# The feed-forward's first two tiles of x loaded, normalised and quantised inside the preparation of the matrices, on one core of Trainium2

## The reference, cut to what matters

```python
mod = (silu(c) @ wmod).reshape(2, 6, 1, -1)
sa, ca, ga, sb, cb, gb = (mod[:, i] for i in range(6))
gb = (2 * (gb >= 0) - 1) * maximum(abs(gb), 0.25)
...                                            # attention: x = x + ga * attn(...)
h = layernorm(x) * (1 + cb) + sb
x = x + gb * ffn(h, w_gate, w_up, w_down)

def fp4_quant_dequant(x):                      # blocks of 16 along the last axis
    scale = maximum(max(abs(xb)) / 6.0, 1e-12)
    return grid[searchsorted(mid, abs(xb / scale))] * sign(xb) * scale

def fp4_linear(x, w):
    return einsum('bsk,nk->bsn', fp4_quant_dequant(x), fp4_quant_dequant(w))

def ffn(x, w_gate, w_up, w_down):
    gate, y = fp4_linear(x, w_gate), fp4_linear(x, w_up)
    return fp4_linear(silu(gate) * y, w_down)
```

## Time and profile before

| | us |
|---|---|
| median of 3 runs | 4038.29 (4036.18 to 4048.62) |
| the profiled execution's own time | 4013.47 |
| its span, first to last instruction | 4011.7 |
| preparation of the matrices, in its span | 2453.0 to 2578.5 |
| first product of the loop | 2599.71 |
| mean granted TensorE clock | 0.966 |

### The profile page before, as it was taken

One profiled execution on the slowest core, in us unless ns is written; L12 is line 12 of the kernel. 1 busy time (PEld: TensorE's weight loads), 2 busy tenths in 40 slices (PEclk: granted clock), 3 DMA queues, 4 the chain that ended last, 5 costly groups with the idle time before them and its releaser, 6 DMA issues. The chain is left out here.

```text
span 4011.7 us, 151421 instructions
## 1 busy us (share of the span) xinstructions
PE 3637.0 (91%) x63808; PEld 2365.8 (59%) x63808; DVE 3342.2 (83%) x7592; ACT 1742.8 (43%) x3510; POOL 863.6 (22%) x687
## 2 busy tenths in 40 slices
PE   4999999999999999999999984099999999999998
PEld 3777767777777676676776762044444444444443
DVE  4788888787888888888888867689999999999997
ACT  2444434434445354443443523344444444444443
POOL 1121222122222221222212210022222222222221
PEclk7999999999999999999999997599999999999999
DMA  4000000000000000100000013322333333333322
GB/s 122 13 25 29 20 25 29 19 30 24 25 30 19 25 29 20 34 20 25 30 19 25 24 71 108 69 72 76 85 87 75 89 82 80 89 75 86 85 77 76
DMA packets 359968, 204.57 MB, mean 51 GB/s; under 512 B 299761, under 2 KB 300401, under 8 KB 359281
## 3 DMA queue, kind: packets, MB, share of 16 engines
q1 hardware_dynamic: 359280, 194.66, 17.7%
HBM read 89.49 MB, written 33.55 MB: 31 GB/s over the span
## 5 line engine op out<-in xcount | busy, mean ns | idle before, releaser
L1618 PE MATMUL fbank<-gT,xqT 128*128 128x464 f16 (+1 forms) x2304 | 491.2, 363 | 124.7 <-DMA xqT<-xq 123.6
L950 DVE COPY_PREDICATED Am<-pick,banks 128x64 f32<-128x64 uint8 (+2 forms) x1792 | 461.7, 258 | 127.4 <-DVE Am L950 12.3
L782 POOL TENSOR_TENSOR raw_up<-raw_up,raw_gate 128x1024 f32<-128x1024 f32 x128 | 315.6, 2466 | 1160.5 <-DVE raw_up L832 1160.5
L1618 PE MATMUL fbank<-uT,xqT 128*128 128x464 f16 (+1 forms) x2304 | 487.7, 361 | 0.0
L1627 PE MATMUL fbank<-dT,hqT 128*128 128x512 f16 x2112 | 469.2, 381 | 8.2 <-DMA hqT<-hq 8.2
L535 PE MATMUL banks<-raw_up,raw_gate 128*128 128x256 f32 x2048 | 456.8, 381 | 2.3 <-DVE xxx L845 2.3
L1618 PEld LDWEIGHTS fbank<-gT,xqT 128*128 128x128 f16 x2304 | 221.8, 98 | 373.2 <-DMA xqT<-xq 117.2
L535 PEld LDWEIGHTS banks<-raw_up,raw_gate 128*128 128x128 f32 x2048 | 389.2, 191 | 67.8 <-issue 17.0
L1618 PEld LDWEIGHTS fbank<-uT,xqT 128*128 128x128 f16 x2304 | 225.4, 98 | 230.9
L1627 PEld LDWEIGHTS fbank<-dT,hqT 128*128 128x128 f16 x2112 | 207.1, 98 | 257.7 <-DMA hqT<-hq 8.5
L436 PE MATMUL banks<-rcol,kvar 32*32 32x80 f32 x8192 | 335.2, 236 | 25.9 <-issue 25.7
(11 more groups left out here) (225 smaller groups left out, 7118.2 us busy)
## 6 DMA issues: line engine op xcount, KB each, us to landing
raw_scale<-in_L_attn_x SPq DMA_DIRECT2D x32, 512.0 KB, 3.6
xres<-in_L_attn_x SPq DMA_DIRECT2D x32, 512.0 KB, 3.6
x_after_attention<-xres SPq DMA_DIRECT2D x32, 512.0 KB, 2.8
xl<-x_after_attention SPq DMA_DIRECT2D x64, 256.0 KB, 2.7
xr<-x_after_attention SPq DMA_DIRECT2D x64, 256.0 KB, 2.6
out<-xr SPq DMA_DIRECT2D x64, 256.0 KB, 2.3
raw_gate<-in_L_ffn_w_gate SPq DMA_DIRECT2D x1, 2816.0 KB, 11.7
raw_up<-in_L_ffn_w_up SPq DMA_DIRECT2D x1, 2816.0 KB, 18.7
```

Of the source, the lines that this page charges most:

```text
L782: nc.gpsimd.tensor_tensor(xf[:, j % NXF].rearrange("p g b t -> p (g b) t"), xf[:, j % NXF].rearrange("p g b t -> p (g b) t"), hT[:, :, :, ...
L950: nc.vector.copy_predicated(dst, mask, src).then_inc((done or A_step).sem, 1)
L1618: last = nc.tensor.matmul(GU[2 * pair + t][:, 0:w], xqT[:, u, a, g, :], W[:, b_, g, lo_:hi_], start=(k == 0), stop=(k == 3 * G - 1))
```

## The change

The first steps of tiles 0 and 1 move from the loop's block into the preparation's block, into each engine's order there. The tiles of x get places in rows of `raw_gate` and `raw_up` that are no longer read at that point, as the preparation's temporary tiles are still in use. The whole preparation moves behind the functions it now calls, so the plain diff shows it as removed and added; what differs is this. VectorE's two copies of c also move behind the first two divisions of gate.

```diff
-        xl = sb("xl", [P, 2, C])
-        passed = sb("passed", [P, C])
-        hx, mx = sb("hx", [P, C]), sb("mx", [P, C])
...
+        xl, hx, passed, mx = early.gate[:, G:G + 2], early.gate[:, G + 2], early.gate[:, G + 3], early.gate[:, G + 4]
+        full_x = early.gate[:, G + 5].bitcast(F16).rearrange("p (a n) -> p a n", a=2)
+        xq = early.gate[:, G + 6].bitcast(F16).rearrange("p (a n) -> p a n", a=2)
+        xqT = early.up[:, 2 * G:2 * G + 2].rearrange("p r n -> p (r n)").bitcast(F16).rearrange("p (u a g t) -> p u a g t", u=2, a=2, g=G)
+        q16x = early.up[:, 2 * G + 2].bitcast(F16)[:, 0:C]
...
 # preparation, SP, behind the transpose of item n
+                        if n == KF - 1:
+                            sp.wait_ge(a_done.sem, KF)
+                            for u in range(2):
+                                sp.dma_start(xl[:, u], x1[u, 0:P, :]).then_inc(xl_loaded[u].sem, 16)
+                        if n == 2 * KF - 2:
+                            sp_xT(sp, 0, 0)
 # preparation, ScalarE, item n
+                        if n == 2 * KF:
+                            act_grid(act, 0, xstep, hx[:], mx[:], xgrid_done)
+                            act_full(act, 0, C, s16x, xs_done, full_x, xfull_done, xlow_done)
...
+                        if n == KF + 4:
+                            act_stats(act, 0, 0, 0)
+                        if n == KF + 6:
+                            act_ln(act, 0, 0)
+                            act_stats(act, 0, 1, 1)
+                        if n == 2 * KF + 1:
+                            act_ln(act, 1, 1)
 # preparation, GpSimd
+                    pool.wait_ge(consts.sem, 1)
                     for t in range(3):
+                        if t == 2:
+                            pool.wait_ge(row_done.sem, 2)
+                            pool_x(pool, 0, 0)
                         pool.wait_ge(wmax_done.sem, t + 1)
                         nc.gpsimd.partition_all_reduce(wall[:, t:t + 1], wmax[:, t:t + 1], P, bass.bass_isa.ReduceOp.max).then_inc(all_max.sem, 1)
+                    pool_x(pool, 1, 1)
 # preparation, VectorE
-                    dve.wait_ge(c_ready.sem, 1)
-                    for b in range(B):
-                        last = V.tensor_copy(c_b[:, b], c_s[:, :, b:b + 1].to_broadcast([P, G, P]))
-                    last.then_inc(cb_ready.sem, 1)
+                    def spread_c():
+                        dve.wait_ge(c_ready.sem, 1)
+                        for b in range(B):
+                            last = V.tensor_copy(c_b[:, b], c_s[:, :, b:b + 1].to_broadcast([P, G, P]))
+                        last.then_inc(cb_ready.sem, 1)
...
                             if t == 2:
+                                dve_xa(dve, 0, 0)
                                 dve.wait_ge(modf_done.sem, 6)
                                 gate_of(V, row_gb, mod_bank[2], ...)
+                                dve_xq(dve, 0, 0)
                             scales(t)
                             for m in range(lead(n)):
                                 scaled(n + m)
+                            if t == 0:
+                                spread_c()
 # loop's block
-                for u in range(2):
-                    sp.dma_start(xl[:, u], x1[u, 0:P, :]).then_inc(xl_loaded[u].sem, 16)
-                run(sp, body, lambda sp: sp_xT(sp, 0, 0))
+                run(sp, body)
                 def first(pool):
-                    pool_x(pool, 0, 0)
                     pool_und(pool, 0, 0)
-                    pool_x(pool, 1, 1)
                 def first(dve):
-                    dve_xa(dve, 0, 0)
-                    dve_xq(dve, 0, 0)
                     dve_h(dve, 0, 0, 0)
                 def first(act):
-                    act_stats(act, 0, 0, 0)
-                    act_ln(act, 0, 0)
-                    act_stats(act, 0, 1, 1)
-                    act_grid(act, 0, xstep, hx[:], mx[:], xgrid_done)
-                    act_full(act, 0, C, s16x, xs_done, full_x, xfull_done, xlow_done)
-                    act_ln(act, 1, 1)
                     act_silu(act, 0, 0, 0)
```

More of the change, by code:

```diff
@@ L1330, in feed_forward @@
+        q16x = early.up[:, 2 * G + 2].bitcast(F16)[:, 0:C]
         sums, ve, rstd = sb("sumsf", [P, 2, 2]), sb("vef", [P, 2]), sb("rstdf", [P, 2])
-        passed = sb("passed", [P, C])
         negmu, nmr = sb("negmuf", [P, 2]), sb("nmrf", [P, 2])
-        hx, mx = sb("hx", [P, C]), sb("mx", [P, C])
-        q16x, q16h = sb("q16x", [P, C], F16), sb("q16h", [P, I_FF], F16)
-        sx, ix = sb("sxf", [P, 5, NBX]), sb("ixf", [P, NBX])
-        sh, ih = sb("shf", [P, 5, NBH]), sb("ihf", [P, NBH])
@@ L1337, in feed_forward @@
-        s16x, s16h = sb("s16x", [P, 2, NBX], F16), sb("s16h", [P, 2, NBH], F16)
-        full_x, full_h = sb("full_x", [P, 2, C], F16), sb("full_h", [P, 2, I_FF], F16)
-        xp, hp = sb("xp", [P, 2, 4]), sb("hp", [P, 2, 4])
-        xq = sb("xq", [P, 2, C], F16)
-        hq = sb("hq", [P, 2, I_FF], F16)
-        xqT = sb("xqT", [P, 2, 2, G, P], F16)
-        hqT = sb("hqT", [P, 2, 2, KF, P], F16)
-        sil = sb("sil", [P, 2, 480])
-        h = sb("h", [P, 2, I_FF])
-        mh = sb("mh", [P, I_FF])
@@ L1347, in feed_forward @@
-        xr, tmpo = sb("xr", [P, 2, C]), sb("tmpo", [P, C])
-        und, head = sb("und", [P, 2, 3]), sb("head", [P, 2])
+        sx = early.up[:, 2 * G + 2, C // 2:C // 2 + 5 * NBX].rearrange("p (k n) -> p k n", k=5)
+        ix = early.up[:, 2 * G + 2, C // 2 + 5 * NBX:C // 2 + 6 * NBX]
+        s16x = early.up[:, 2 * G + 2, C // 2 + 6 * NBX:C // 2 + 7 * NBX].bitcast(F16).rearrange("p (k n) -> p k n", k=2)
+        xp = sb("xp", [P, 2, 4])
         xl_loaded = [sig(f"xl_loaded{u}", 1, 16) for u in range(2)]
@@ new lines, in feed_forward @@
+        q16h = sb("q16h", [P, I_FF], F16)
+        sh, ih = sb("shf", [P, 5, NBH]), sb("ihf", [P, NBH])
+        s16h = sb("s16h", [P, 2, NBH], F16)
+        full_h = sb("full_h", [P, 2, I_FF], F16)
+        hp = sb("hp", [P, 2, 4])
+        hq = sb("hq", [P, 2, I_FF], F16)
+        hqT = sb("hqT", [P, 2, 2, KF, P], F16)
+        sil = sb("sil", [P, 2, 480])
+        h = sb("h", [P, 2, I_FF])
+        mh = sb("mh", [P, I_FF])
+        xr, tmpo = sb("xr", [P, 2, C]), sb("tmpo", [P, C])
+        und, head = sb("und", [P, 2, 3]), sb("head", [P, 2])
```

346 lines of the change are left out of this document (173 added, 173 removed).

## The result

The changed kernel took 4022.23 us in the median of 8 runs (4007.89 to 4027.5), the kernel before 4039.89 beside it (4032.66 to 4048.62): a ratio of 0.9955 (95% interval 0.9941 to 0.9969). The forecast was 4026.1, the range 4019 to 4035. The profiled execution took 4021.98 us, span 4020.1. The one of before had taken 4013.47: its attention, which the change doesn't touch, had ended 25 us sooner (the preparation's first memset at 2453.05 against 2478.53). So whole spans of single executions aren't compared here. The feed-forward is, counted from that memset and in one profiled execution of each kernel, in three stretches: to the loop's first product, from there to the first product of the last tile (63 distances), and the rest.

A forecast was written before the change was run, and what follows sets the result against it. TensorE was taken to set the feed-forward loop's pace, so the question was when its first product starts. The terms 21.0 - 5.8 + 0.5 - 3.5 = 12.2 us gave a median of 4026.1 us, range 4019 to 4035.

The forecast's parts named there:

- Step 1: Tail of the preparation: TensorE can start tile 0's first product at the release; 21.0 us gained.
- Step 2: Tile 0's division and quantisation on VectorE, now ahead of the last matrix's scales; 5.8 us paid back.
- Step 3: Head of the preparation: moved copies of c start the scales earlier, limited by the first all-reduce; 0.5 us gained.
- Step 4: Preparation: ScalarE's and GpSimd's work for the two tiles delays VectorE; 3.5 us paid net, bounds 0 and 6.2.
- Part (c): End of the preparation: VectorE's waits of 0.52 and 0.63 us for transposes shrink; 1.1 us back.
- Step 5: Other configuration changes, tile 0's und and TensorE's clock cost nothing.
- Rival D: Loop: another phase of GpSimd's meetings makes tiles wait for xqT; 13.3 us more, 4039.4; 8%.
- B: Preparation: GpSimd's meetings cost little or the first load is short; 14 to 19 us gained, about 4022; 22%.
- C: Preparation: GpSimd's code loads are paid at the first call; 3.4 us gained in all, 4034.9; 13%.
- E: Preparation: tile 0's x isn't through GpSimd when VectorE reaches its division, so VectorE waits; about 4037; 4%.

The follow-up runs named there:

- the copies alone: The kernel before with only VectorE's two copies of c moved behind the first two divisions of gate; 4038.66 us in a single execution.
- the late division: The changed kernel with tile 0's normalisation behind the last scales of up and its division behind the gate row; 4017.82 us, ratio 0.9951.
- the added power: The changed kernel with one more GpSimd power, on other data, right behind the second all-reduce; 4025.95 us in a single execution.

## Why the prediction was right in its number, point by point

**Step 1, 21.0 us: right.** It measured 21.13 (21.17 less 0.04).

**Step 2, 5.8 us: right.** The division ran 2558.07 to 2560.21, the quantisation 2566.39 to 2570.00, 5.75 together.

**Step 3, 0.5 us: right.** 0.37 with the copies alone. Its bound of 3.8 is excluded: wmax was early, but VectorE stood 3.30 us ahead of the bit mask until the all-reduce had come.

**Step 4, 3.5 us: the step that failed; 6.04 measured,** just inside its bound of 6.2. (The release came 11.42 later; less the 5.75 of step 2, plus the 0.37 of step 3.) The step put it as "The two exclude each other, at 1.1 us of VectorE per wide operation, 2.2 per tile". They exclude each other, but VectorE doesn't take turns: in unbroken two-operand work GpSimd mostly waits for its first gap. So tile 0's wide operations cost nothing that shows, and tile 1's the 0.5 us of the last parts. What cost was the small power, priced at nothing beyond its load. Held 6.99 us, it stalled ScalarE and through it VectorE by 5.55 us. VectorE's waits in the preparation, without those at the first scales, sum to 9.86 us after the change and 3.93 before, which is 5.93 of the 6.04. Part (c) fell in half: of the two waits for transposes that were to shrink, 0.52 went into the stall, the other didn't (0.64 at the end, 0.63 before), and tile 0's two loads in SP's queue, priced at nothing, seem to have made one of them 1.08 instead of 0.37 (0.36 with the copies alone, which leave the loads where they were). On this the cited rule was weighed wrongly: the Trainium skill has another sentence, on "SBUF — State Buffer" (section SBUF: two separate sides), by which a VectorE operation with two inputs in memory also takes the shared pair, and whoever starts first keeps it for the whole instruction. The rows agree: in the late division GpSimd had begun 0.05 us ahead and held a part for 1.49 us. What they add is that the next VectorE instruction can beat a GpSimd one that has waited through eight of them. It doesn't always: tile 1's power ended after 1.04 us (0.62 in the late division) between two wide VectorE operations with no gap in the timeline. VectorE's records otherwise overlap by 0.08 us, and there they only touch, so a pause of that size seems to be enough.

**Step 5: the configuration changes and und at nothing: right** (the third all-reduce came 0.14 us behind its maximum). That the loop would stay as it was is what failed, by 7.7 us. Rival D named the right thing, "another phase of GpSimd's meetings", with the wrong sign and by another cause: not the start, but the load's alignment moved the phase. The mean tile went from 21.71 to 21.58 us. That is net of a small loss at the loop's start: from tile 1's first product to tile 2's it takes 24.12 us, 22.74 before, so not all that follows the first product moved with it. Waits for xqT, D's sign, fell from 9.4 to 6.1 us (2725 to 3965 us, 14 times).

Luck made the total good. Two errors of opposite sign, 2.5 us too few of cost and 7.7 us too few of gain, left the number 3.9 us too high (4026.1 against 4022.2); by gains, 12.2 were forecast and 17.1 to 17.7 measured. B's time (4022) was met, but not its reason: in the preparation the gain was smaller than forecast. C had the path of the cost right (a late power, ScalarE standing at the normalisation, VectorE without row 18's scales, 6.4 us forecast and 5.55 measured), but not its cause: the power of tile 0 began 0.16 us behind its operand, with no load ahead of it. E didn't happen: tile 0's x was through GpSimd at 2551.7, before VectorE's division.

## What to carry to other kernels

When GpSimd shares data or time with a VectorE that works without gaps, ask first who waits for GpSimd's smallest operation: it may not be done until VectorE pauses, so place it where nobody queued behind it is needed. A one-source VectorE operation there may help too, as GpSimd began undisturbed beside the reduction of h, but no run tried it. When a tile's address changes, compare the transfers' medians, and compare the phase in which GpSimd's operations meet VectorE's short ones: here a shift of 0.2 us was worth 15 us of 1367, more than the 9.7 of the moved steps. And look for the gain where the bounding engine waits, here TensorE's hand-over between tiles. Last, read a gain stage by stage, since a right total can be the sum of two wrong terms.

## What the runs showed of the hardware that was not expected

- A GpSimd operation of one element per partition took 0.55 us in the loop, 6.96 to 8.87 beside VectorE's unbroken two-operand work, ending 0.41 to 0.46 us behind the start of its first pause in all seven kernels where ScalarE's operand came in such work (and yet the added power took 0.62 in it); one of 128x512 took 11.86 instead of 1.27. VectorE's operations kept their lengths meanwhile.
- VectorE's reduction, with one input, runs undisturbed beside GpSimd (1.62 us), while its one-input scaling of 88 columns in f32 is held (0.21 to 1.19 us) if GpSimd has begun 0.01 to 0.14 us ahead, and is safe if it has itself begun first.
- 128 bytes off a multiple of 256, the 256 KB load of x took 3.1 us instead of 2.7, a store 2.8 instead of 2.3, and h's transposes 3.7 instead of 3.2; the residual's load, shifted too, kept its 2.7.
- SP is busy 3.3 us with the issue of one transpose of `parts` in the down rows, and the next left only behind it, though its operand had been ready for 1 us (in the run with tile 1's wide operations late).
- A ScalarE copy of 0.2 us a tile that nobody reads shortened a loop bound by TensorE by 1.1%.
